# Asking for a small transfer before twelve large ones: a reordered DMA queue and a denominator inverted and spread earlier on VectorE

## The reference, cut to what matters

```python
q = taylor_feature_map(q)          # 16 heads, 16 features each
k = taylor_feature_map(k)
kv = cumsum(k[..., None, :] * v[..., :, None], axis=2)
y = einsum('bhtD,bhtdD->bhtd', q, kv)
z = cumsum(k, axis=2)
denom = sum(q * z, axis=-1, keepdims=True) + EPS
y = y / denom
...
return y @ Wo.T
```

## Time and profile before

| | |
|---|---|
| time, median of 3 runs | 3643.65 us (3641.67 to 3645.97) |
| the profiled execution | 3645.97 us, its span 3644.0 us |
| PE busy | 3498.8 us, 96% of the span |
| ACT busy | 2684.7 us, 74% |
| DVE busy | 2593.9 us, 71% |
| POOL busy | 1217.7 us, 33% |
| mean granted clock of TensorE | 0.988 of full speed |

### The profile page before, as it was taken

How to read it: one execution, slowest core, us unless ns; L and a number is a source line. 1 busy time by engine, 2 the same in 40 slices (tenths; PEclk the granted TensorE clock), 3 DMA queues, 4 the chain that set the end, 5 groups by cost and what they waited for, 6 DMA issues and landing times.

```text
span 3644.0 us, 88007 instructions
## 1 busy us (share of the span) xinstructions
PE 3498.8 (96%) x32736; PEld 2436.4 (67%) x32736; DVE 2593.9 (71%) x8128; ACT 2684.7 (74%) x5852; POOL 1217.7 (33%) x1191
## 2 busy tenths in 40 slices
PE   7999999998589999999999999999999999999997
PEld 3443344443367777777777777777777777777776
DVE  3555555564477877778787877878787787878774
ACT  6778887778367777777777777777777777777774
POOL 2222111221333433334343343434333333433432
PEclk9999999999799999999999999999999999999999
DMA  7554666554312222222222222222222222222220
GB/s 181 122 108 99 123 117 128 119 95 68 138 51 69 56 63 65 61 64 56 67 61 65 60 56 71 57 66 60 60 68 61 65 56 66 62 65 60 56 54 22
DMA packets 269210, 277.31 MB, mean 76 GB/s; under 512 B 38768, under 2 KB 202864, under 8 KB 268144
## 3 DMA queue, kind: packets, MB, share of 16 engines
q1 hardware_dynamic: 268784, 271.68, 31.4%
HBM read 97.23 MB, written 50.33 MB: 40 GB/s over the span
## 4 chain that ended last, share of the span: by engine, by line
PE 43%; DVE 16%; issue 7%; SPq 4%; DMA 3%; POOL 2%; ACT 0%; DVEq 0%; POOLq 0%
PE f_ps L1339 10%; PE f_ps L1443 9%; PE f_ps L1455 5%; PE f_ps L1420 5%; DVE pr L1108 4%; PE f_ps L1344 3%; PE f_ps L1364 2%; DVE cosine L1058 2%; PE f_ps L1401 2%; DMA xsh<-x 2%; DVE act_u L1154 2%; DVE ssq L1066 2%; PE f_ps L1382 2%; DVE pr L1091 2%; PE f_ps L1411 1%
## 5 line engine op out<-in xcount | busy, mean ns | idle before, releaser
L1258 ACT ACTIVATE pr<-pr,nmax,rnorm 128x192 f32<-128x192 f32 x1024 | 545.9, 534 | 346.3 <-DVE nmax L1098 346.3
L1339 PE MATMUL f_ps<-wqkv_s,hT 128*128 128x512 f32 x1536 | 716.8, 603 | 11.3 <-ACT hT L1220 5.9
L1443 PEld LDWEIGHTS f_ps<-hnT,w_s 128*128 128x128 f32 x5120 | 593.9, 193 | 60.4 <-issue 58.8
L1443 PE MATMUL f_ps<-hnT,w_s 128*128 128x128 f32 x5120 | 595.3, 276 | 0.8 <-DVE hnT L1144 0.8
L520 ACT ACTIVATE weights<-t_ps,four_s 128x1024 f32<-128x1024 f32 x576 | 580.0, 1301 | 6.0 <-PE t_ps L628 5.7
L985 POOL TENSOR_TENSOR rstd<-ve,f_mhalf 128x1 f32<-128x1 f32 x128 | 81.5, 637 | 1122.4 <-DVE ve L1132 1122.4
L1108 DVE TENSOR_SCALAR pr<-pr,rsum 128x192 f32<-128x192 f32 x1024 | 449.8, 500 | 9.0
L1339 PEld LDWEIGHTS f_ps<-wqkv_s,hT 128*128 128x128 f32 x1536 | 272.4, 190 | 270.6 <-issue 246.2
L997 POOL TENSOR_TENSOR turned<-qk,rot 128x256 f32<-128x256 f32 x512 | 396.2, 798 | 55.4 <-ACT qk L1225 41.8
L1091 DVE CUSTOM_DVE_ANT_0 pr<-f_ps,mask 128x192 f32<-128x192 f32 x1024 | 326.3, 355 | 68.0 <-PE f_ps L1371 66.0
L383 DVE SCALAR_TENSOR_TENSOR weights<-weights,causal_s 128x512 f32<-128x512 f32 x192 | 164.0, 868 | 281.9 <-ACT weights L520 281.2
(11 more groups left out here) (122 smaller groups left out, 6492.7 us busy)
## 6 DMA issues: line engine op xcount, KB each, us to landing
vw<-vw SPq DMA_DIRECT2D x628, 128.0 KB, 2.4
qkT<-parts_dram SPq DMA_DIRECT2D x384, 128.0 KB, 5.8
kT<-kT SPq DMA_DIRECT2D x124, 256.0 KB, 2.6
parts_dram<-parts SPq DMA_DIRECT2D x64, 384.0 KB, 2.8
xs<-x_dram SPq DMA_DIRECT2D x8, 1024.0 KB, 7.9
xn_dram<-xn SPq DMA_DIRECT2D x8, 1024.0 KB, 5.4
attn_dram<-ao SPq DMA_DIRECT2D x8, 1024.0 KB, 10.6
xin<-xn_dram SPq DMA_DIRECT2D x64, 128.0 KB, 2.2
```

What stands on the lines that cost most here:

```text
L1258: last = a.activation(chances(h), chances(h), ACT.Exp, bias=nmax[:, h:h + 1], scale=rnorm[:, h:h + 1], accum_out=psum[:, h:h + 1])
L1339: last = mm(ps[:, b, :], rows, wqkv_s[:, l, c, i * INNER:(i + 1) * INNER], start=(c == 0), stop=(c == KC - 1))
L1443: last = mm(ps[:, UP[j // 2], o:o + P], w1_s[:, l, c, half * FULL + j * P:half * FULL + j * P + P], hnT[:, c, :], start=(c == 0), stop=(c ...
```

## The change: what it does

On SyncE, `invert(b, g)` is put ahead of `load_heads(b, g + 2)`. On VectorE, in each group g of 1 and more, `invert_den(b, g - 1)` goes from behind `mask_diagonals(g, 4)` to right behind `mask_diagonals(g, 2)`, and `spread_den(b, g - 1)` goes from the end of the group to the place that `invert_den` had, right behind `mask_diagonals(g, 4)`. No operation is added or removed.

```diff
             for b in range(B):
                 for g in range(GROUPS - 1):
+                    invert(b, g)
                     if g + 2 < GROUPS:
                         load_heads(b, g + 2)
-                    invert(b, g)
...
                     mask_diagonals(g, 2)
+                    if g >= 1:
+                        invert_den(b, g - 1)
                     if following is not None:
...
                     mask_diagonals(g, 4)
                     if g >= 1:
-                        invert_den(b, g - 1)
+                        spread_den(b, g - 1)
                     if following is not None and g >= 2:
                         for t in range(2, 4):
                             layer_norm(following, (g - 2) * TILES // 2 + t)
                     add_before(g, 0)
                     mask_diagonals(g, 7)
                     mask_diagonals(g, 8)
-                    if g >= 1:
-                        spread_den(b, g - 1)
```

## The result

The changed kernel takes 3745.09 us (median of 4, 3741.94 to 3751.31) against 3644.17 us (median of 4, 3641.67 to 3645.97) for the kernel before. The ratio is 1.0276, 95% interval 1.0265 to 1.0289, so +101 us. The forecast was 3733 us, range 3691 to 3758. The changed kernel's profiled execution has a span of 3744.5 us, 100.5 us more than before.

The account below looks back on a forecast made before the run. ScalarE's squares were taken to bound the attention stage. Stalls of 56.8 us plus 35.2 us of half clock less 2.5 us at the end gave +89.5 us, 3733 us in terms of the median, range 3691 to 3758.

Parts of the forecast that it names:

- The place and the sign: Attention stages: late qkT loads stall TensorE, then ScalarE, twice in each of 8 sequences; slower, chance 0.93.
- The steps of SyncE's order: SyncE, group 1: reciprocal without wait, return transfer, then first load at group start + 8.2 us, 10.5 us later than before.
- the time of a set: Twelve qkT loads, first issue to last landing: 12.9 us taken, from a span of 12.6 to 13.4.
- the stall without the clock's part: ScalarE at each late set: 3.55 us, bounds 3.1 and 4.1, 16 times, 56.8 us.
- The clock: TensorE behind each stall: half clock costs 2.2 us more, bounds 0 and 3.2, 16 times, 35.2 us.
- VectorE's order: Earlier reciprocal and spread: hidden within a group; normalise starts sooner in the last sequence, -2.5 us once.
- Rival A: TensorE behind the stalls: same stall but the clock stays up, +54.3 us, 3698 us; chance 0.15.
- Rival B: qkT loads land in time, within 8.5 us; only the end's 2.5 us gained, 3641 us; chance 0.04.
- Rival C: Between sequences: loads in time and earlier normalise gives 2.5 us at each of 8 ends, 3624 us; chance 0.03.
- Rival D: Small transfers land late, VectorE and SyncE's loads slip; each us costs 16 us; chance 0.05, shared with longer half clock.

Follow-up runs that it names:

- busy pause: Changed kernel plus 5 extra matmuls on TensorE ahead of the wait for the loads of groups 2 and 3: 3711.06 us, ratio 1.0188.
- GpSimd's queue: Kernel before with VectorE's new order and both small transfers issued by GpSimd, SyncE's loads at the old place: 3693.36 us, ratio 1.0144.

## Why the prediction was right

**The place and the sign** were right. The late loads of groups 2 and 3 are the loss: 16 waits of TensorE for qkT, 16 pairs of gaps of ScalarE. The loss follows the time at which the loads are asked for. At 4.6 us into the group ScalarE lost up to 1.5 us for a set, at 8.3 us 4.3 us with the clock kept up, at 12.4 us a first gap of 8.8 us, and with half of the set ahead nothing.

**The steps of SyncE's order** held: reciprocal with no wait, return transfer 3.7 us after the first, first load at 8.3 us (8.2 forecast). **The term that was mis-sized** is the time of a set. It was put at 12.9 us, between 12.5 and 13.4, from three sets of the kernel before. The 16 late ones took 13.0 to 14.4, 13.7 in the mean, and 13 of them were over that upper bound. TensorE's pauses were therefore 4.9 us in the mean and not 4.4, and the stall without the clock's part was 4.3 us (busy pause), not 3.55, and over its own bound of 4.1. That is 16 x 0.8 = 13 us, enough for the 12 by which the forecast fell short. The range held nonetheless, because the other bound in it, 3.2 us of clock loss for a stall, was far from being reached. In that it was lucky. By the landing of the last load, the same 16 sets took 13.0 us in the mean in the kernel before, and 13.4 in the changed one (there read for 12 of them). Why they take longer there, no run shows.

**The clock** cost 2.1 us for each set by the busy pause, against 2.2 forecast. The pauses of 4.4 and 4.6 us were answered by half clock though all my three rows were over 5 us, and so was the one of 1.93 us in the kernel of VectorE's order alone. Rival A is out. The Trainium skill (TensorE: Matmul & The Clock Gate, "Why this matters for your kernels") says to leave no gaps between bursts of matmuls. The runs agree: filling the pause kept the clock at 1.00, where it had been 0.71 and 0.79.

**Rival B** needed the loads within 8.5 us, and no set took less than 13.0.

**VectorE's order** cost nothing in the changed kernel and gave 2.6 us at the end, against 2.5. Between sequences an earlier `normalise` gave nothing, as said: from the last square of a sequence, 241.73 + 16.18 = 257.91, to the next stage's first at 295.28 it is 37.37 us, and before 269.67 - 232.30 = 37.37. Rival C is out with B. Rival D didn't occur in the changed kernel, but its mechanism is real: it is what slowed the kernels of VectorE's order alone and of GpSimd's queue.

The forecast missed that VectorE and GpSimd slow each other. They do so in the kernel before too, where it costs ScalarE nothing:

```profile
221.42 2.78 DVE L313 TENSOR_SCALAR xn<-xs,t_mv,t_rstd 128x256 f32<-128x256 f32 x2
```

These two layer norms stand beside GpSimd's sum (220.44 to 223.72). The new order moves the meeting to where masks are due. In the changed kernel no loss from it is seen. With the clock kept up (busy pause), ScalarE has no gap inside an attention stage but the one ahead of each late set, apart from four of up to 0.5 us near the start of two stages. The slow masks are there (two take 3.44 us, 232.46 to 235.90), but TensorE stands until 237.55 for qkT anyway, so the late loads hide them.

No version beats the kernel before by more than the measurement can tell.

## What to carry to other kernels

A queue's order is a list of waits as much as of transfers: before a small, urgent item is put ahead of a large prefetch, look for the wait that it contains and count the prefetch's slack (here 6.4 us spare, 10.5 us taken). If the order must change, split the item or the prefetch so that most of the bytes stay ahead of the wait. When the engine that is held up has no idle time of its own, a pause costs its length and then a part again at half clock.

## What the runs showed of the hardware that was not expected

A transfer of 16 KB took 7.6 us in the median on GpSimd's queue beside twelve loads of 128 KB on SyncE's. A pause of TensorE of 1.93 us was followed by a granted clock of 0.50, while one of 2.65 us was not (1.00 over the next 8 us). Two layer norms on VectorE (128x256, fp32, SBUF to SBUF) took 0.64 us alone and 2.79 us beside a GpSimd product of 2.47 us, and two masks 3.88 us where such a pair took at most 1.9 (0.69 and 1.23). The Trainium skill (SBUF — State Buffer, "Terms") describes a pair of ports that VectorE and GpSimd hold by turns for a whole instruction. The added 2.15 us, close to GpSimd's 2.47, agree with that. No run here tells it from another cause of the slowing.
